# A decoder block: whole-matrix loads of the output weights, a quarter turn folded into the step's angle, and a new order of work

## What is computed

```python
# layer 1: a diagonal complex state space model with 32 states
Lam     = -(softplus(Lambda_unconstrained_re) + 1e-4 + 0.01) + 1j * Lambda_im
Lam_bar = exp(Lam * exp(log_Delta[:32]))
B_bar   = ((Lam_bar - 1) / Lam)[:, None] * (B_re + 1j * B_im)
Bu      = einsum('bld,nd->bln', u, B_bar)
xs      = associative_scan(x[t] = Lam_bar * x[t-1] + Bu[t])
y       = 2 * real(einsum('bln,dn->bld', xs, C_re + 1j * C_im)) + D * u
x = layernorm(x + y)
# layer 2: one expert per sequence, both products quantized to int8 with smoothed scales
x = layernorm(x + smooth_quant_mlp(x, gate_up_weight, down_weight))
# layer 3: a router over 8 experts of 176 hidden units, top 2, silu(gate) * up
x = layernorm(x + sum_e share[e] * (silu(h @ G_e.T) * (h @ U_e.T)) @ Down_e.T)
```

## Time and profile before

| | |
|---|---|
| median of 3 runs | 168.07 us (167.99 to 168.33) |
| the profiled execution, its own time | 169.42 us |
| its span, first to last instruction | 167.6 us |
| TensorE busy (matmuls) | 147.6 us, 88% |
| VectorE, ScalarE, GpSimd busy | 110.9, 86.0, 82.9 us |
| moved by DMA | 14.55 MB |

### The profile page before, as it was taken

One profiled execution on the slowest core, in us unless ns is written; L12 is line 12 of the kernel. 1 busy time (PEld: TensorE's weight loads), 2 busy tenths in 40 slices (PEclk: granted clock), 3 DMA queues, 4 the chain that ended last, 5 costly groups with the idle time before them and its releaser, 6 DMA issues.

```text
span 167.6 us, 3392 instructions
## 1 busy us (share of the span) xinstructions
PE 147.6 (88%) x1158; PEld 140.4 (84%) x1158; DVE 110.9 (66%) x381; ACT 86.0 (51%) x185; POOL 82.9 (49%) x131
## 2 busy tenths in 40 slices
PE   7308897997699999699999999999999999999980
PEld 7207786786599999599999999999998999999980
DVE  3826498998989859669878858861593633355242
ACT  7321059878777778445666674438217332152301
POOL 4701048979793936912374466204386315424512
PEclk9955899999999999999999999999999999999997
DMA  4399996000000064100256100044500015420101
GB/s 108 106 291 309 392 359 218 7 2 0 2 4 2 19 152 144 35 0 2 66 153 142 25 0 31 6 113 140 126 4 0 31 29 164 121 68 4 33 0 63
DMA packets 13285, 14.55 MB, mean 87 GB/s; under 512 B 1716, under 2 KB 13012, under 8 KB 13012
## 3 DMA queue, kind: packets, MB, share of 16 engines
q1 hardware_dynamic: 13268, 14.34, 28.7%
HBM read 13.25 MB, written 1.08 MB: 85 GB/s over the span
## 4 chain that ended last, share of the span: by engine, by line
PE 58%; DVE 12%; POOL 8%; DMA 8%; SPq 5%; issue 4%; ACT 3%; POOLq 0%; ACTq 0%; DVEq 0%
PE ps_gu L352 9%; PE ps_gu L357 9%; PE ps_gu L353 9%; DMA u_feat<-in_xT 6%; PE ps_out L373 5%; PE ps_out L374 5%; PE ps_out L377 5%; SPq L277 3%; DMA gu_raw<-share_rows 2%; PE ps_ab L386 2%; POOL gu_raw L1181 2%; POOL rs L1138 2%; POOL gu_lo L1167 2%; PE ps_ab L391 1%; POOL rs L1141 1%
## 5 line engine op out<-in xcount | busy, mean ns | idle before, releaser
L352 PE MATMUL ps_gu<-x_hi,gu_hi 128*128 128x256 f32 x176 | 47.3, 291 | 0.0
L353 PE MATMUL ps_gu<-x_hi,gu_lo 128*128 128x256 f32 x176 | 45.5, 281 | 0.0
L1181 POOL TENSOR_TENSOR gu_raw<-gu_raw 128x512 f32<-128x512 f32 (+1 forms) x24 | 28.9, 1209 | 29.6 <-DVE gu_raw L1568 24.9
L357 PE MATMUL ps_gu<-x_lo,gu_hi 128*128 128x256 f32 x176 | 35.3, 282 | 0.0
L352 PEld LDWEIGHTS ps_gu<-x_hi,gu_hi 128*128 128x128 f32 x176 | 33.1, 188 | 0.2
L353 PEld LDWEIGHTS ps_gu<-x_hi,gu_lo 128*128 128x128 f32 x176 | 33.2, 188 | 0.1
L357 PEld LDWEIGHTS ps_gu<-x_lo,gu_hi 128*128 128x128 f32 x176 | 27.0, 188 | 0.0
L1568 DVE TENSOR_TENSOR gu_raw<-sil,ps_gu 128x512 f32<-128x512 f32 (+1 forms) x24 | 15.3, 639 | 12.5 <-PE ps_gu L357 8.5
L373 PE MATMUL ps_out<-dp_hi,hid_hi 128*128 128x256 f32 x77 | 20.9, 293 | 0.2 <-DVE u_feat L1582 0.2
L808 ACT ACTIVATE hid_hi<-gu_raw 128x512 fp32r<-128x512 f32 (+1 forms) x24 | 14.0, 591 | 12.2 <-POOL gu_raw L1181 11.7
L789 ACT ACTIVATE sil<-ps_gu 128x512 f32<-128x512 f32 (+1 forms) x24 | 13.4, 557 | 12.8 <-PE ps_gu L357 12.8
(11 more groups left out here) (265 smaller groups left out, 318.2 us busy)
## 6 DMA issues: line engine op xcount, KB each, us to landing
gu_raw<-in_guT SPq DMA_DIRECT2D x1, 2824.0 KB, 13.6
gu_raw<-share_rows SPq DMA_DIRECT2D x16, 128.0 KB, 3.3
dp_raw<-in_dpT SPq DMA_DIRECT2D x1, 1408.0 KB, 16.3
u_feat<-in_xT SPq DMA_DIRECT2D x4, 256.0 KB, 7.3
w_feat<-in_wT SPq DMA_DIRECT2D x4, 256.0 KB, 10.5
out<-u_feat SPq DMA_DIRECT2D x8, 128.0 KB, 1.7
gu_raw<-share_rows SPq DMA_DIRECT2D x8, 112.0 KB, 2.9
gu_raw<-share_rows SPq DMA_DIRECT2D x8, 96.0 KB, 3.0
```

Source lines behind the costliest of these rows:

```text
L352: pe.matmul(dst, gu_hi[:, c, kind, col], x2_hi[:, b % 2, c], start=(c == 0), stop=False)
L353: pe.matmul(dst, gu_lo[:, c, kind, col], x2_hi[:, b % 2, c], start=False, stop=False)
L357: last = pe.matmul(dst, gu_hi[:, c, kind, col], x2_lo[:, b % 2, c], start=False, stop=(c == DC - 1))
L1181: pool.tensor_tensor(hid[:, lo:hi], hid[:, lo:hi], shares[:, lo:hi], ALU.mult).then_inc(hid_ready, 1)
```

## The change

The output matrices are loaded whole, 128 rows from row 0 on, one contiguous pattern each. The four groups of rows therefore stand in another order than before. For the two groups where real and imaginary parts have changed place, ScalarE computes the step's sine and cosine a quarter turn on (the first 64 partitions: minus the sine in the cosine's column, the cosine in the sine's), and signs and offsets become columns of the tile `signs`, which GpSimd's `factors` reads. That makes four small activations of two, and four more memsets on VectorE. The count and kind of all other instructions stay.

All the lists are put into another order. On TensorE the small steps (transposes, the expert's products, the router) stand in fewer and longer groups between `gate_up` and `down`.

```diff
-        signs = sb("signs", [P, 4])
+        signs = sb("signs", [P, 5])
...
-            for raw, rows in ((c1_raw, c1), (c2_raw, c2)):
-                sp.dma_start(raw[:], bass.AP(rows.tensor, HALF * D, [[HALF * D, 2], [D, 2 * HALF], [1, D]])).then_inc(l_c, 16)
+            sp.dma_start(c1_raw[:], c1).then_inc(l_c, 16)
+            sp.dma_start(c2_raw[:], c2).then_inc(l_c, 16)
...
             def step_angles():
+                ahead, even = slice(0, 2 * HALF), slice(2 * HALF, P)
                 act.wait_ge(step_ready, 1)
-                act.activation(sv[:, 15:16], sv[:, 10:11], ACT.Sin, scale=TWO_PI)
+                act.activation(sv[ahead, 14:15], sv[ahead, 10:11], ACT.Sin, scale=-TWO_PI)
+                act.activation(sv[even, 15:16], sv[even, 10:11], ACT.Sin, scale=TWO_PI)
                 act.wait_ge(step_abs_ready, 1)
-                act.activation(sv[:, 14:15], sv[:, 13:14], ACT.Sin, scale=-TWO_PI,
-                               bias=half_pi[:]).then_inc(step_trig_ready, 1)
+                act.activation(sv[ahead, 15:16], sv[ahead, 13:14], ACT.Sin, scale=-TWO_PI, bias=half_pi[ahead])
+                act.activation(sv[even, 14:15], sv[even, 13:14], ACT.Sin, scale=-TWO_PI,
+                               bias=half_pi[even]).then_inc(step_trig_ready, 1)
...
-                pool.tensor_scalar(column(20), column(14), column(7), -1.0, ALU.mult, ALU.add)
-                then(pool.tensor_scalar(column(21), column(15), column(7), 1.0, ALU.mult, ALU.mult))
+                pool.wait_ge(signs_ready, 1)
+                pool.tensor_scalar(column(20), column(14), column(7), signs[:, 2:3], ALU.mult, ALU.add)
+                then(pool.tensor_scalar(column(21), column(15), column(7), signs[:, 4:5], ALU.mult, ALU.add))
...
+                dve.memset(signs[0:half_turn, 2:3], 0.0)
+                dve.memset(signs[half_turn:P, 2:3], -1.0)
+                dve.memset(signs[0:half_turn, 4:5], -1.0)
+                dve.memset(signs[half_turn:P, 4:5], 0.0)
                 for g in range(G4):
-                    sign = 1.0 if g in (0, 3) else -1.0
-                    dve.memset(signs[g * HALF:(g + 1) * HALF, 1:2], -sign * TWO_PI)
-                    last = dve.memset(signs[g * HALF:(g + 1) * HALF, 3:4], sign)
+                    dve.memset(signs[g * HALF:(g + 1) * HALF, 1:2], TWO_PI if g == 2 else -TWO_PI)
+                    last = dve.memset(signs[g * HALF:(g + 1) * HALF, 3:4], -1.0 if g % 2 == 0 else 1.0)
...
             x1_norm(0, 1)
+            gate_up_hi(0)
             router_split()
-            gate_up_hi(0)
             gate_up_hi(1)
+            gate_up_hi(2)
+            smooth_x(0, 0)
             smooth_w(0)
-            smooth_x(0, 0)
-            gate_up_hi(2)
+            gate_up_hi(3)
             x1_norm(1, 0)
```

More of the change, by code:

```diff
@@ L603, in _ @@
             state_in(3)
+            wq_transpose(2)
             gate_up(0, 5, 0)
-            down(0, 0, 0)
+            gate_up(0, 5, 1)
             x2_transpose(1)
-            gate_up(0, 5, 1)
             state_out(3, 0)
+            state_out(3, 1)
+            router(1)
             expert_in(2)
-            router(1)
-            state_out(3, 1)
             gate_up(1, 0, 0)
+            gate_up(1, 0, 1)
+            gate_up(1, 1, 0)
+            gate_up(1, 1, 1)
             share_transpose(1)
-            down(0, 0, 1)
@@ L642, in _ @@
             down(0, 1, 5)
-            gate_up(1, 4, 0)
+            gate_up(1, 4, 1)
+            xq_transpose(3)
             x2_transpose(2)
-            gate_up(1, 4, 1)
+            wq_transpose(3)
             gate_up(1, 5, 0)
+            gate_up(1, 5, 1)
+            down(1, 0, 0)
+            router(2)
             scale_broadcast(3)
-            gate_up(1, 5, 1)
             expert_in(3)
-            router(2)
-            down(1, 0, 0)
             down(1, 0, 1)
             down(1, 0, 2)
+            gate_up(2, 0, 0)
@@ L962, in _ @@
             x2_hi_first(1)
-            down_hi(2)
             unround_w(1)
+            gate_up_hi(6)
+            gate_up_hi(7)
             silu(0, 0)
             expert_silu(1)
+            gap_tanh(0)
             smooth_x(2, 0)
+            smooth_w(2)
+            silu(0, 1)
             smooth_x(2, 1)
-            gap_tanh(0)
-            gate_up_hi(7)
-            smooth_w(2)
+            smooth2_w(1)
             share_copy(0)
-            smooth2_w(1)
-            silu(0, 1)
+            quant_d(1)
@@ L1001, in _ @@
+            silu(1, 1)
+            x1_norm(3, 1)
+            smooth2_w(2)
             share_copy(1)
-            silu(1, 0)
-            smooth2_w(2)
-            x1_norm(3, 0)
-            x1_norm(3, 1)
             quant_d(2)
+            smooth_w(3)
             quant_a(2)
-            silu(1, 1)
+            smooth_x(3, 0)
+            silu(1, 2)
+            unround_both(2)
+            smooth_x(3, 1)
             rows2_copy(2)
-            smooth_w(3)
-            smooth_x(3, 0)
-            smooth_x(3, 1)
```

339 lines of the change are left out of this document (166 added, 173 removed).

## The result

Measured: **162.47 us** median of 4 runs (160.73 to 163.4), before 168.2 us (167.99 to 169.54); the ratio is 0.961, with a 95% interval of 0.951 to 0.971. The forecast was 163.4 us, its range 159.8 to 166.2. The profiled execution takes 162.29 us, with a span of 160.5 us.

The account below looks back on a forecast made before the run. TensorE's own work was taken to bound the kernel from 47.5 us, a chain of waits behind a late load before that. Start -3.9, clock +0.5, large stage -1.3 took 168.07 to 163.4 us; range 159.8 to 166.2.

Parts of the forecast that it names:

- The loads: Start: output matrices go on sixteen DMA engines instead of two, landing by 6 to 6.5 us, `u_feat` 1 behind them.
- The first statistics: Start, records of L426 and L431: begin at 12.1 to 13.7 us for 19.11, so -6.3 us (-5.4 to -7.0).
- `gu_raw`: Load ahead of ScalarE's splits: lands at 19.5 us, then 8.7 us to `expert_in(0)` at 28.2, so -3.9 of the -6.3.
- The clock: TensorE waiting from about 19 to 22.5 us may drop to half clock: +0.5 us, bounds 0 and +1.5.
- From 32.1 to 47.5 us: Between the expert's start and the large stage: same steps in nearly the same places, 0 within 0.7 us either way.
- The large stage: From 47.5 us on: the 1.49 us wait before `x2_transpose(1)` goes, 0.2 for new waits; -1.3 us (0 to -2.2).
- Small steps beside each other: TensorE's grouping in the large stage: no price found for switching between transposes and `gate_up` products, so worth 0.
- C: Slower: `gu_raw` still lands at 22.95 us, TensorE's clock falls, small steps take twice as long; 169.4 us, chance 0.05.
- A: The start decides alone: `gu_raw` lands by about 16.5 us, all of the 6.3 stays; 160.5 us, chance 0.22.
- B: Given back later: the new order opens waits in the large stage; 166.2 us, up to 167.5, chance 0.10.
- D: The loads still go on two engines, only the order is left; 167 to 168 us, chance 0.03.
- E: Longer groups of transposes make TensorE's clock fall, costing 5.1 us; 168.5 us, chance 0.02.

Follow-up runs that it names:

- two_engines: The changed kernel with its two output matrices read from the same rows by a pattern written in three sizes, the outermost two; 161.58 us, ratio 0.957.
- after_again: The changed kernel measured once more without any edit, on another chip; 161.66 us, ratio 0.961.
- keep_warm: The changed kernel with 24 products of ones instead of 4 ahead of the first expert transposes; 162.42 us, ratio 0.968.
- norm_first: The kernel before with only GpSimd's `rstd2(1)` moved one share product earlier; 169.14 us, ratio 1.004.
- gu_split: The changed kernel with `gu_raw` loaded by two DMAs, router and three experts first, the rest on its own semaphore; 159.84 us, ratio 0.949.
- warm_start: gu_split with six products of ones on TensorE between `state_in(0)` and `state_in(1)`; 159.28 us, ratio 0.947.
- inputs_first: The changed kernel with ScalarE's first smoothing steps and GpSimd's first inverse deviation ahead of the splits, some splits later; 161.83 us, ratio 0.964.

## Why the prediction was right, and where it wasn't

The time and the sign were right, and the forecast's case was the one that came: the chain moved from `u_feat` to `gu_raw`. Step by step:

*The loads.* Right: the hole fills (0.85), `c_raw` lands after 3.3 us. The reason given, two engines of sixteen by the outermost size, holds in its direction (0.13, 0.46, 0.84 for 2, 4, 16), with the reservation that contiguous halves count as one piece. The reading of 0.13 as two of sixteen was in part luck: the same pattern gives 0.09 and 0.20 in two other executions. The rule of the Trainium skill (page "DMA: Bandwidth & Descriptors", section "Why a DMA increments its semaphore by 16 and not by 1") agrees with the order of the three shares, though not with their sizes as a count. The section takes the pattern as the instruction carries it, and adds that software may split a contiguous pattern so that it uses all engines; two_engines behaves that way, though no run shows the instruction's own pattern.

*The first statistics.* -7.2 in the profile of the changed kernel, just beyond the -7.0 of my bound, and -5.6 in the one of after_again. The whole spread is the clock's. The added activations cost 0.05 us, the factors being ready at 8.34 us for 8.29.

*`gu_raw`*, the term of the sum that was mis-sized: I put it at 19.5 us, it landed at 18.1 (17.7 in after_again). I had carried the 316 GB/s of the earlier trace rows over and added 1.3 us for a lag. But those 316 GB/s were measured with the two engines' queue still in them; without it the stretch moves 378 GB/s. That rate is the error, not the lag: 0.55 MB by 4.5 us and 0.63 MB by 7 us leave 3.68 MB of the 4.86, which take 9.6 us at the 382 GB/s of 7 to 18.1 us, so to 16.6; the load landed 1.5 us behind that. From the landing on, 8.7 us were predicted and 8.5 measured at the full clock.

*The clock.* The late fall did come in the first profile, and cost 1.06 us for my 0.5; in after_again it didn't. I had taken it for a property of the kernel, but of its two profiles one has it early, where `gu_raw` hides it, and one late, on the path. I take that for a part of the 2.7 us by which the changed kernel's runs scatter; which of the other runs had which isn't recorded, and keep_warm scatters by 1.9 us at a nearly full clock. The kernel before does something alike: its runs at a mean clock of about 0.98 and of about 0.963 differ by 0.9 us in the mean, its profiled execution, from which I made the sum, was of the latter kind, and so the 7.1 us between the two profiles are more than the 5.7 between the medians. That the forecast came within 1 us of the median is therefore in part luck: `expert_in(0)` gained 1.0 us more than my -3.9 + 0.5 and the large stage 1.4 us more than my -1.3, but I took the sum off the median, 1.35 us below the execution that I had made it from.

*From 32.1 to 47.5 us*: 0 was right, 15.39 us in both.

*The large stage*: -2.7 us measured, -1.3 predicted, with -2.2 as the bound. Two errors in it. That the wait of 1.49 us goes was right, but not by the step I named: `rstd2(1)` alone gives nothing (norm_first). By the rows ScalarE's list has to change with GpSimd's; no run moves just these two. And I set the rest of the idle time at nothing gained and 0.2 lost, while it went too. The distances between the starts of TensorE's records say how much there was: in the profile of before they are 1.71 us too long at 71.08 us, 0.60 at 127.6, 0.42 at 110.9 and 0.41 at 67.1, 3.1 us in all, of which the brackets had shown 2.2, because a record is longer than its place in the pipe. In the profile after the change about 0.45 are left in all, spread over many records.

*Small steps beside each other.* Worth 0, as predicted. The number of passages between small and large products goes from 64 to 34. Around each one the four distances between starts add up to what they are elsewhere, with a median difference of 4 ns from small to large and -4 from large to small before the change, 1 and -12 after it; only a passage from the router's products costs 0.09 us, and one of three of those is saved. By these distances the changed order helps because it takes waits away, not because it groups; no run has the one without the other.

*The rivals.* C needed a landing of 21.4 us or later. Its mechanism (TensorE idle behind `gu_raw`, then half the clock) did appear in part, for 1.06 us. A was wrong for the changed kernel and became nearly true when `gu_raw` was split: gu_split at 159.84 and warm_start at 159.28 us, for A's 160.5. B's "given back later" is what inputs_first did. D and E did not happen: the stage from 43.1 us on is at a clock of 1.00 with all its longer groups of transposes. Whether transposes count as work for the clock can't be seen there, since large products stand between the groups.

## What to carry to other kernels

A small load with a poor pattern costs more than its bytes: here everything issued behind it on the queue was late, and a large load late in the list arrived last. When such a hole is filled, ask at once which load the strict list of an engine waits for next, and whether that engine needs all of it: two DMAs with a semaphore each gave 1.8 us more in the median here without moving a step, and the gain hangs on the clock's early fall staying away.

In kernels whose lists are written by hand, a wait belongs to all the lists at once. Before moving one step, read on every engine what stands ahead of the step that is waited for. And measure waits of a pipelined engine by the distances between starts, not by the idle brackets alone.
